# A two-layer recurrent block on one core: opening, slots, first shift and queue order rebuilt

## The reference, cut to what matters

```python
x = L0_attn_x                                     # [2, 1024, 128]
xn = layernorm(x)
s = attention(xn, L0 weights)                     # 16 heads of 8, rotary, causal, softmax
g = silu(soft_moe(xn))                            # rmsnorm, 8 experts x 64 slots, dispatch and combine softmax
x = x + s * g
xn = layernorm(x)
s = attention(xn, L1 weights)
g = silu(layernorm(xn + expert_choice_moe(xn)))   # 16 experts, top-2 mask, best 512 tokens for each expert
x = x + s * g
```

## Time and profile before

| | us |
|---|---|
| median of 3 runs | 819.37 |
| lowest, highest | 805.48, 820.41 |
| the profiled execution | 810.94 |
| its span, first to last instruction | 809.1 |
| mean granted TensorE clock in it | 0.878 |

### The profile page before, as it was taken

One profiled execution on the slowest core, in us unless ns is written; L12 is line 12 of the kernel. 1 busy time (PEld: TensorE's weight loads), 2 busy tenths in 40 slices (PEclk: granted clock), 3 DMA queues, 4 the chain that ended last, 5 costly groups with the idle time before them and its releaser, 6 DMA issues.

```text
span 809.1 us, 14402 instructions
## 1 busy us (share of the span) xinstructions
PE 688.0 (85%) x5166; PEld 328.1 (41%) x5166; DVE 512.5 (63%) x844; ACT 450.7 (56%) x896; POOL 286.5 (35%) x488
## 2 busy tenths in 40 slices
PE   3337868999979999899989999999999997999944
PEld 1125612355555336443332364334434333256613
DVE  7872398876544572577646547698899897653301
ACT  1214303655636676866656765676767774645841
POOL 3548512233100111267421114672122122015883
PEclk9558955999998999698788997899999997799965
DMA  5200563020370123003341124055132212000000
GB/s 160 68 10 1 155 169 116 28 60 27 103 188 7 35 51 78 10 1 92 122 112 43 47 61 152 2 139 147 46 86 60 56 32 61 1 1 2 1 26 27
DMA packets 33476, 52.24 MB, mean 65 GB/s; under 512 B 5888, under 2 KB 24064, under 8 KB 30848
## 3 DMA queue, kind: packets, MB, share of 16 engines
q1 hardware_dynamic: 32112, 50.87, 23.3%
q10 hardware_dynamic: 1296, 0.46, 0.2%
HBM read 37.42 MB, written 13.63 MB: 63 GB/s over the span
## 4 chain that ended last, share of the span: by engine, by line
PE 60%; DVE 16%; POOL 10%; issue 6%; ACT 5%; DMA 2%; POOLq 0%; SPq 0%; ACTq 0%; DVEq 0%
PE ps L1184 55%; DVE maxes L1170 6%; ACT probs L922 3%; DVE rope L1034 2%; POOL gate L462 2%; PE ps L1390 1%; DMA F<-in_w 1%; PE ps L1277 1%; POOL gate L799 1%; POOL gate L810 1%; ACT F L882 1%; POOL gate L811 1%; PE ps L1238 1%; DVE kop L1039 1%; PE ps L1293 1%
## 5 line engine op out<-in xcount | busy, mean ns | idle before, releaser
L1170 DVE TENSOR_REDUCE maxes<-ps 128x2 f32<-128x1024 f32 (+2 forms) x288 | 339.9, 1221 | 116.2 <-PE ps L1184 114.1
L922 ACT ACTIVATE probs<-ps 128x512 f32<-128x512 f32 x576 | 306.0, 603 | 119.4 <-PE ps L1184 118.6
L1184 PE MATMUL ps<-qop,kop 74*128 74x512 bf16 (+3 forms) x768 | 193.0, 351 | 13.8 <-ACT probs L922 7.0
L775 POOL TENSOR_SCALAR_AFFINE_SELECT probs<-probs 128x512 f32<-128x512 f32 (+1 forms) x160 | 83.5, 544 | 264.3 <-ACT probs L922 264.0
L1184 PE MATMUL ps<-probs,vgrp 128*32 128x512 f32 (+3 forms) x1536 | 160.2, 528 | 12.8 <-POOL probs L775 11.3
L1184 PE MATMUL ps<-kmx,qmx 32*128 32x128 bf16 (+2 forms) x1280 | 109.7, 282 | 27.5 <-DVE maxes L1170 14.8
L1184 PEld LDWEIGHTS ps<-qop,kop 74*128 74x128 bf16 x768 | 62.9, 103 | 119.5 <-ACT probs L922 60.3
L1184 PE MATMUL ps<-F 128*128 128x128 f32 (+3 forms) x768 | 93.5, 285 | 6.1 <-DMA F<-in_w 3.3
L1184 PEld LDWEIGHTS ps<-F 128*128 128x128 f32 (+2 forms) x768 | 85.6, 185 | 24.8 <-issue 16.3
L1184 PEld LDWEIGHTS ps<-kmx,qmx 32*128 32x128 bf16 x1280 | 39.1, 94 | 135.2 <-issue 77.0
L1184 PEld LDWEIGHTS ps<-probs,vgrp 128*32 128x32 f32 x1536 | 39.2, 113 | 73.9 <-issue 53.1
(11 more groups left out here) (154 smaller groups left out, 685.9 us busy)
## 6 DMA issues: line engine op xcount, KB each, us to landing
qop<-q_thirds SPq DMA_DIRECT2D x48, 192.0 KB
kop<-k_thirds SPq DMA_DIRECT2D x48, 192.0 KB
qmx<-q_thirds SPq DMA_DIRECT2D x16, 256.0 KB
kmx<-k_thirds SPq DMA_DIRECT2D x16, 256.0 KB
F<-in_w SPq DMA_DIRECT2D x16, 256.0 KB, 5.0
q_thirds<-third SPq DMA_DIRECT2D x8, 384.0 KB, 3.0
k_thirds<-third SPq DMA_DIRECT2D x8, 384.0 KB, 2.8
q_thirds<-third SPq DMA_DIRECT2D x8, 256.0 KB, 2.2
```

Of the source, the lines that this page charges most:

```text
L775: last = pool.affine_select(where, where, [[0, number], [1, P]], ALU.is_ge, 0.0, base=0, channel_multiplier=-1)
L922: act.activation(probs[:, u % RING, :], bank(at), ACT.Exp, scale=SCALE).then_inc(s_cells_read, 1)
L1170: dve.tensor_reduce(dst, src, AX.X, ALU.max).then_inc(s_units_read[pair // 2], 1)
L1184: return pe.matmul(out_, lhsT, rhs, start=first, stop=last)
```

## The change

What it does, by part:

- **Opening.** `root` of layer 0 is made once for chunks 0 and 1 (on DVE) and once for 2 and 3 (on POOL). `xr` is four ACT copies with a scale; gamma is applied as the scale of the `xrT`, `embT` and `slot` copies. `rope` has a buffer for each parity of the chunk and a single `sine`; layer 0's `sum` runs on DVE. The memsets of `kop` and `qop` (rows 64 to 127) run on POOL ahead of everything.
- **Exponentials.** The `exp` product takes all 128 rows of `kop` and `qop`; the added ones meet zeros.
- **First shift by halves.** `PATTERN` has the six units of the first 512 queries in front. In groups 0 and 8 `top`, `halve`, `shift` run for each half (`parts`), and `exp` unit 0 waits for the first half alone.
- **Whole slots.** `slot` is one piece of 8 products of 128 columns.
- **Values.** `pv` reads `vals` directly with 9 columns a head; `vgrp` goes, bank 7 is cleared once.
- **Split pieces.** The exponentials of `lt` and `lg` are pieces of their own, `soft` and `comb`; the pair of banks stays taken until they ran. `colsum`, `rden` and `halve` are pieces; `heads` runs by halves. The adds of layer 1's chunks 2 and 3 run on DVE.
- **Order.** The planner has a model of TensorE's clock, other prices, and a table `MORE` that is added to `tail`.

```diff
+LAST = ((1, 2), (1, 3))
-PATTERN = [[(i, 0, 512)] for i in (4, 5, 6, 7)] + [
-    [(2, 0, 256), (3, 0, 256)], [(6, 512, 256), (7, 512, 256)],
-    [(1, 0, 128), (3, 256, 128), (5, 512, 128), (7, 768, 128)],
-    [(i, P * i, 128) for i in range(4)], [(i, P * i, 128) for i in range(4, 8)]]
+PATTERN = [[(2, 0, 256), (3, 0, 256)], [(1, 0, 128), (3, 256, 128), (5, 512, 128), (7, 768, 128)],
+           [(i, P * i, 128) for i in range(4)]] + [[(i, 0, 512)] for i in (4, 5, 6, 7)] + [
+    [(6, 512, 256), (7, 512, 256)], [(i, P * i, 128) for i in range(4, 8)]]
+SPLIT = (0, 8)
+UNITS_DONE = {0: 6, 1: NM, 2: NM}
...
[...]
+WEIGHT = {"max": 0.25, "shift": 0.25}
+MORE = {
+    "add": (6, -26), "attT": (-5, -4), "colsum": 11, "comb": 16, "count": -1, "disp": 26, "emb": 3, "embT": -27,
+    "embstat": -78, "eo": -2, "es": -16, "halve": (11, -3), "heads": (4, 22), "hid": 7, "hid1": -2, "high": (-59, -3),
...
-    "slot": (0.92, "A", (("ACT", 0.25),)), "hid": (1.04, "A", (("ACT", 1.5),)), "eo": (1.7, "D", (("DVE", 0.43),)),
+    "slot": (1.96, "A", (("ACT", 0.27),)), "hid": (1.04, "A", (("ACT", 1.5),)), "eo": (1.7, "D", (("DVE", 0.43),)),
...
     if kind == "root":
-        return [("stat", L, c)]
+        return [("stat", L, c)] if L else [("stat", L, 2 * c), ("stat", L, 2 * c + 1)]
...
     if kind == "qk":
         before = (L, c - 1) if c else (L - 1, 3)
-        return [("v", L, c)] + ([("low",) + before + (arg[2],)] if before[0] >= 0 else [])
+        same = (L, c - 2) if c >= 2 else (L - 1, c + 2)
+        return [("v", L, c)] + ([("sum",) + before + (arg[2],)] if before[0] >= 0 else []) + (
+            [("low",) + same + (arg[2],)] if same[0] >= 0 else [])
...
+            pool.memset(kop[64:P].rearrange("p r h t -> p (r h t)").bitcast(F32), ONES).then_inc(s_ones, 1)
+            pool.wait_ge(s_ones, 1)
+            pool.memset(qop[64:P].rearrange("p r h t -> p (r h t)").bitcast(F32), 0.0).then_inc(s_ones, 1)
...
-                elif kind == "xr":
-                    c, = arg
-                    four = slice(4 * c, 4 * c + 4)
-                    pool.wait_ge(s_f0, 48)
-                    pool.wait_ge(s_norm, NTH["norm", 0, c, 3])
-                    for t in range(4 * c, 4 * c + 4):
-                        last = pool.tensor_scalar(xr[:, t, :], xn[:, t, :], root[:, 1, 1, t:t + 1], None, ALU.mult)
-                    own.link(last)
-                    pool.tensor_tensor(xr[:, four, :], xr[:, four, :], gam0[:, 0:1, :].to_broadcast([P, 4, E]),
-                                       ALU.mult).then_inc(s_xr, 1)
...
+                    for t in range(4 * c, 4 * c + 4):
+                        last = act.activation(xr[:, t, :], xn[:, t, :], ACT.Copy, scale=root[:, 1, 1, t:t + 1])
...
+                elif kind == "sum" and not arg[0]:
+                    L, c, n = arg
+                    made = UNIT["qk", L, c, n]
+                    dve.wait_ge(s_units_read[made % 2], made // 2 + 1)
+                    dve.tensor_tensor(rope[:, c % 2, n, :], rope[:, c % 2, n, :], sine[:, n, :], ALU.add).then_inc(s_summed[0], 1)
                 elif kind == "embstat":
-                    for r in range(2):
-                        dve.memset(kop[64:KM, r], 1.0).then_inc(s_ones, 1)
...
                     for i in range(TB):
-                        last = mm(bank(at)[:, 0:SL0], xr[:, u // NB0 * TB + i, :], disp[:, u % 2, i, SL0 * half:SL0 * half + SL0],
-                                  i == 0, i == TB - 1)
+                        last = mm(quarter(at, 0), xr[:, u // NB0 * TB + i, :], disp[:, u % 2, i, :], i == 0, i == TB - 1)
...
-                        last = mm(bank(at)[:, c:c + w], kop[0:KM, r, h, P * j:P * j + P], qop[0:KM, r, h, q:q + w])
+                        last = mm(bank(at)[:, c:c + w], kop[:, r, h, P * j:P * j + P], qop[:, r, h, q:q + w])
...
-                            last = mm(ps[VP * h:VP * h + VP, 7, q % BANK:q % BANK + w], vgrp[:, n % 2, j, h, :],
+                            last = mm(ps[VP * h:VP * h + VC, 7, q % BANK:q % BANK + w], vals[:, n // GB % 2, j, n % GB * HG + h, :],
```

More of the change, by code:

```diff
@@ L17 @@
 import concourse.bass as bass
+import math
 import numpy as np
@@ L304, in streams @@
         made.append([("store", L, c) for c in range(4)])
+    made += [[("root", 0, pair)] for pair in range(2)]
     made += [[("xr", c), ("xrT", c)] for c in range(4)]
@@ L332, in streams @@
     made.append([("out", n, half) for n in groups for half in range(2)])
-    made.append([("heads", L, b) for L in range(2) for b in range(B)])
+    made += [[(kind, L, b, half) for L in range(2) for b in range(B)] for half in range(2) for kind in ("rden", "heads")]
     made.append([("attT", L, c) for L in range(2) for c in range(4)])
@@ L378, in schedule, with run @@
             stack.pop()
+    granted, worked = [0.5], [0.0]
+    def run(at, us, weight):
+        while us > 1e-9:
+            k = int(at / WINDOW)
+            while len(granted) <= k:
+                granted.append(1.0 if worked[-1] >= (KEEP if granted[-1] == 1.0 else REGAIN) else 0.5)
+                worked.append(0.0)
+            part = min(us / granted[k], (k + 1) * WINDOW - at + 1e-9)
+            worked[k] += part * weight / WINDOW
+            us -= part * granted[k]
+            at += part
+        return at
+    tail = {what: long + more(what) for what, long in tail.items()}
+    held = {}
     order, done, last = [], {}, {what: takers[-1][0] if takers else "PE" for what, (_, _, takers) in price.items()}
@@ L426, in schedule @@
         if ring:
-            rings[ring].append(end)
+            held[what] = len(rings[ring])
+            rings[ring].append(math.inf if kind in LATER else end)
+        elif kind in LATER.values():
+            first_use = next((k,) + what[1:] for k in LATER if LATER[k] == kind)
+            rings["D"][held[first_use]] = end
         if takers and takers[0][0] == "SP" or kind == "shift":
@@ L442 @@
         UNIT[what] = len(UNIT)
-    NTH[what] = 1 + sum(w[0] == what[0] for w in NTH)
+    same = 2 if what[0] == "sum" else 1
+    NTH[what] = 1 + sum(w[:same] == what[:same] for w in NTH)
 def summed(n, step):
@@ L739, in _ @@
                     pool.wait_ge(s_stat, NTH["stat", L, c])
-                    refine(pool, own, *(root[:, 0, n, 4 * c:4 * c + 4] for n in range(3)))
+                    own.link(refine(pool, own, *(root[:, 0, n, 4 * c:4 * c + 4] for n in range(3))))
                 elif kind == "norm" and arg[0]:
@@ L794, in _ @@
+                    pool.tensor_tensor(att[:, four].rearrange("p i g c -> p (i g) c"),
+                                       raw[:, four, :, :, 0:D].rearrange("p i g h c -> p (i g h) c"),
+                                       rden[:, four].rearrange("p i g h -> p (i g h)").unsqueeze(2).to_broadcast(
+                                           [P, 4 * GB * HG, D]), ALU.mult).then_inc(s_heads, 1)
+                elif kind == "add" and arg not in LAST:
                     L, c = arg
```

382 lines of the change are left out of this document (237 added, 145 removed), and 1 row of the table COST.

## The result

| | before | after |
|---|---|---|
| median of 5 runs, us | 811.95 | 738.30 |
| lowest, highest | 805.48, 820.41 | 735.88, 741.93 |
| the profiled execution | 810.94 | 741.93 |
| its span | 809.1 | 739.9 |
| mean granted clock | 0.878 | 0.935 |

The ratio of the times is 0.914, 95% interval 0.908 to 0.919; two of before's five runs (819.37 and 820.41) are in a slower state and stay out of it, which is why it isn't that of the medians (0.909). The change makes the kernel 9% faster; the forecast was 756 us, with a range of 722 to 795.

What follows compares the result with a forecast made beforehand. TensorE was taken to set the time from 146 to 760 us, VectorE's and GpSimd's fixed order the opening. Terms 38 + 11 + 8 + 4 = 61 took 810.9 to 750, stated as 756 us; range 722 to 795.

Steps and rivals of the forecast that it cites:

- The step from 750 to 756: Whole kernel: the profiled forecast of 750 us, scaled by before's median 819.4 over 810.9 to 758, stated as 756.
- Work: TensorE's work counted at full clock over the whole span: near 603 us after, from 616 before.
- Opening, 38 us forecast: First 146 us: the state before had at 146 comes at 107; taken 38 us, bounds 10 and 46.
- The chain to the first maximum: Opening: moments, transposes, rotations, sums and stores allow the first row-maximum product at 44 to 52 us instead of 99.17.
- rival P: Opening: VectorE and GpSimd lock each other out at the port, memsets included; 16 us less gain, 766 to 774; chance 0.06.
- rival B: Opening doesn't come forward: GpSimd's or VectorE's queue has the mixture's work ahead of splitting; 787 by profile, 794 median; chance 0.22.
- Slots, 11 forecast: Slot units: 16 products of 128 columns save 1.6 us for each of 8 units, 12.8; taken 11, bounds 8 and 14.
- Full height, 8 forecast: Exponential products, 146 to 760 us: 128 rows instead of 74 cut half clock's 40 us; taken 8, bounds 0 and 20.
- The order, 0 forecast: All queues: the planner's clock model, prices and offsets change every order; plus or minus 10 us, taken 0.
- The end, 4 forecast: Closing stretch: adds on VectorE 1.1 us, heads by halves 1.5, the mask's wait 0 or 8; taken 4, bounds 2 and 11.
- Rival D: Mixture's maxima: separate exponentials keep a PSUM pair taken, so maxima stop and the kernel is slower; 830 us, chance 0.04.
- A: Whole kernel: the forecast itself, 750 to 765 us around its terms, own range 735 to 780; chance 0.55.

Runs made afterwards that it cites:

- experiment 3: The changed kernel, same order, with each slot piece as 16 products of 64 columns again: 742.2 us, ratio 0.910.
- experiment 4: The changed kernel with the table of priorities at zero, clock model and prices kept, so every queue's order changes: 784.0 us, ratio 0.962.
- experiment 2: The kernel before, own order kept, with the exponential's products widened from 74 to 128 rows: 790.4 us, ratio 0.969.
- experiments 8 and 12: 8: the changed kernel with first shift whole, 735.4 us; 12: that plus one opening memset on VectorE and first-shift transfers from ScalarE's queue, 738.9 us.
- experiment 1: The changed kernel, same order, with the exponential's products over 74 rows again instead of 128: 748.3 us, ratio 0.912.

## Why the prediction was right, and where its steps were not

The direction, the mechanism "less idle time and less half clock around the same work" and the sum held: 61 us forecast by the profiled execution, 69 found. The terms are another matter; that their sum came out is luck, since it came out through errors that cancel. The step from 750 to 756 was off too: it scaled by the median of three runs of before, 819.37, and the median of all five is 811.95.

**Work.** 603 us forecast, 605 found. The slot unit was forecast at 2.1 us and takes 2.02.

**Opening, 38 us forecast.** The state before had at 146 was forecast at 107. Before had 63.7 us of work done there, of which 6.4 is four slot units' saving that after doesn't have to do; 57.3 is reached in after at 100 + (57.3 - 44.6) / (34.1 / 46) = 117 us. So the state comes 29 us earlier and not 39, and the 6.4 of slots is in that 29. The chain to the first maximum was forecast at 44 to 52 and ended at 62.6. Two steps failed. The first transpose was put near 13 and came at 16.65: all of this is the memsets, which held two instructions of VectorE for 0.91 and 3.12 us in place of 0.17. I had priced the memsets well (3.51 each, bounds 3.5 to 7) and asked only whether GpSimd itself was free again; rival P carried them at 0.06. The second step is VectorE's order. I had the four rotations run from 18.5 and the second chunk's sums end near 30. VectorE ran moments of chunks 2 and 3 and of the slot embeddings first and began to rotate at 24.49; ahead of the second chunk's sums it normalised chunks 2 and 3 (3.70 us), so they ended at 39.86. GpSimd's own order cost little: its scaling held the first subtraction to 32.5 where the first high part was ready at 30.5, and before the second chunk's it stood idle for 4.3 us and waited for ScalarE. This is rival B's mechanism, a fixed queue with other work ahead, in VectorE's queue and at some 10 us instead of 25. From the second store to the first maximum, 15.6 us against the 16.3 taken over from before, was right.

**Port lock.** The trace shows which forms of VectorE a memset of GpSimd holds: the two TENSOR_SCALARs of 4 columns took 0.91 and 3.12 and ended with a memset, the TENSOR_TENSOR between them, with its two inputs, took 0.16. The Trainium skill (SBUF — State Buffer, "SBUF: two separate sides") says that two SBUF inputs collide only with a GpSimd instruction that reads; the trace agrees, with these 0.16 us beside a memset, against 1.13 beside a reading sum in the earlier trace rows.

**Slots, 11 forecast.** Measured 0 to 4 (experiment 3). The work was saved as computed, but in a stretch where TensorE now waits for a transfer. I had written "hidden where TensorE idles anyway" and then taken 11 of 12.8, by before's idle time and not by after's.

**Full height, 8 forecast, bounds 0 and 20.** Measured 24.6 us in before, and 5 to 10 in after. The direction from the earlier trace rows was right: 13.98 of 14.00 us busy and still at half clock. The size was too small because I bounded it at half of the 40 us and took 8 by feel. Before's stretches from 322 to 520 alone, at 0.84 and 0.87 with TensorE over 92% busy, would have carried more: by an estimate 109.05 x 0.16 + 74.93 x 0.13 = 27 us.

**The order, 0 forecast, plus or minus 10.** This was the worst step. The table alone is worth 40 to 46 us (experiment 4); with the structure but not the table, the kernel is at 784, only 6 us below before with 128 rows (790.4, experiment 2). I said that "the rows can't price it", which was true of the table's numbers but not of what order could be worth: the middle's 80 us of loss with TensorE the busiest engine was in the earlier trace rows, and only half clock and order could be in it.

**The end, 4 forecast, bounds 2 and 11.** 11 us less is lost. Heads by halves (1.08 against 1.96 in the earlier trace rows) and the adds on VectorE (0.69 each) are as forecast. The forecast that value sums would no longer wait 10 us for a mask is half right; the timeline of after:

```profile
721.71 1.90 PE L1317 MATMUL ps<-probs,vals 128*9 128x512 f32 x8 [5.95 <-POOL probs L860]
```

The mask stands behind two products and two adds of GpSimd (from 715.81 to 720.98), 1.26 us each. This is still the largest wait of the end.

**Rival D** (the held pair) didn't happen: no stop of the maxima for an exponential of the mixture is among TensorE's ten largest waits. By the chances, the result lies in A's own range (735 to 780), near its lower end.

The measured terms can't be added up to 69 us: the table, worth 40 to 46, acts in the same middle and end as the rows and the split pieces.

## What to carry to other kernels

When the busiest engine is over 90% busy and its clock isn't at the top, price the order and the shape of its work first: here a table of priorities was worth 40 to 46 us and 128 rows for 74 up to 24.6, and the rebuilt opening brought one state forward by 29. Cost a saved instruction by the idle time that will be there afterwards, not by the idle time of before. Issue small transfers that others wait for from a queue in which no store stands before them, and measure an edit of a planned program knowing that its new order may move the time by 10 us by itself (experiments 8 and 12).

## What the runs showed of the hardware that I had not expected

- The same columns at a height of 128 rows instead of 74 bring TensorE's clock back sooner after a gap: 20.00 of 20 us busy at 0.50 with 74 rows, and at 1.00 with 128, after the same 4.6 us of idle time in sum (experiment 1). It was worth 24.6 us in before and 5 to 10 in after.
- A GpSimd memset of 3.51 us held a VectorE TENSOR_SCALAR of 128x4 for 3.12 us, while a TENSOR_TENSOR with two inputs in SBUF ran beside it in 0.16.
- Transfers of 8 KB landed 1.9 us after their issue by the median of after's 28 ordinary shifts. Those of the first shifts took 5.5 to 6.3 us from issue to release in the opening, and in layer 1 5.4 to 12.6 from the second issue. What makes them longer is open.
